# Gated pass of a graph network: the time angle made in turns by TensorE, the features flipped one superblock later

## What is computed

```
# second layer, per edge
ef = jnp.concatenate([h_src, h[col]], axis=1)
edge_weights = jax.nn.sigmoid(jax.nn.relu(ef @ We1 + be1) @ We2 + be2)[:, 0]
aggr = jax.ops.segment_sum(edge_weights[:, None] * h_src, col, num_segments=n)
# fourth layer, per edge
rel_t = last_update[src] - t
rel_t_enc = jnp.cos(rel_t[:, None] * Wt[0][None, :] + bt)
edge_attr = jnp.concatenate([rel_t_enc, msg], axis=-1)
```

## Time and profile before

| what | us |
|---|---|
| median of three runs | 13408.96 |
| lowest and highest run | 13392.93, 13420.43 |
| profiled execution, span | 13400.0 |
| VectorE busy, whole span | 10400.3 (78%) |
| TensorE busy, whole span | 8527.8 (64%) |
| GpSimd busy, whole span | 6926.8 (52%) |
| ScalarE busy, whole span | 3614.6 (27%) |
| gated pass, first to last keeping of the one-hot (L1505) | 6581.2 to 7974.6 |

### The profile page before, as it was taken

How to read it: one execution, slowest core, us unless ns; L and a number is a source line. 1 busy time by engine, 2 the same in 40 slices (tenths; PEclk the granted TensorE clock), 3 DMA queues, 4 the chain that set the end, 5 groups by cost and what they waited for, 6 DMA issues and landing times. The chain is left out here.

```text
span 13400.0 us, 212567 instructions
## 1 busy us (share of the span) xinstructions
PE 8527.8 (64%) x52858; PEld 6962.8 (52%) x52859; DVE 10400.3 (78%) x15015; ACT 3614.6 (27%) x7819; POOL 6926.8 (52%) x7047
## 2 busy tenths in 40 slices
PE   4663477776777677775465652777266666567764
PEld 3553245554455535654455542555266666566664
DVE  8666569974799748996688875888778888688888
ACT  0111133332333233332244431333211111111111
POOL 2775047750477407772277750777145555255553
PEclk8555688877888788887688875666588888788887
DMA  4334754444544474443255550222233334233333
GB/s 182 113 113 119 244 206 106 106 80 193 192 106 106 72 292 123 106 106 53 79 145 145 146 111 19 55 55 54 19 103 106 107 107 105 75 108 105 105 106 72
DMA packets 720185, 1523.62 MB, mean 114 GB/s; under 512 B 364796, under 2 KB 416585, under 8 KB 680627
## 3 DMA queue, kind: packets, MB, share of 16 engines
q0 software_dynamic: 306624, 795.04, 25.0%
q1 hardware_dynamic: 413427, 727.07, 15.9%
HBM read 1050.48 MB, written 471.10 MB: 114 GB/s over the span
## 5 line engine op out<-in xcount | busy, mean ns | idle before, releaser
L970 POOL DMA_INDIRECT h<-table,edges_ring x3984 | 3856.5, 968 | 1889.0 <-issue 1154.3
L1147 PE MATMUL bank<-h,edges_onehot 128*128 128x260 f32 (+1 forms) x7968 | 1986.6, 406 | 652.3 <-issue 469.0
L1147 PEld LDWEIGHTS bank<-h,edges_onehot 128*128 128x128 f32 x7968 | 1570.6, 246 | 978.1 <-issue 717.4
L970 POOL DMA_INDIRECT edges_rows<-table,edges_ring x1512 | 1527.0, 1010 | 716.0 <-issue 431.0
L1122 PE MATMUL bank<-ident,edges_score 128*4 128x128 f32 x5280 | 1027.7, 360 | 1021.5 <-DVE edges_score L1288 737.9
L1258 DVE TENSOR_TENSOR_SCAN bank<-edges_fresh,edges_top,bank 4x1024 f32<-4x1024 bf16 x660 | 1541.5, 2336 | 144.9 <-PE bank L1122 141.2
L1265 DVE TENSOR_TENSOR_SCAN edges_top<-edges_fresh,bank 4x1024 f32<-4x1024 bf16 x660 | 1493.8, 2263 | 0.6 <-issue 0.3
L1122 PEld LDWEIGHTS bank<-ident,edges_score 128*4 128x4 f32 x5280 | 497.6, 104 | 1339.0 <-DVE edges_score L1288 784.9
L1314 DVE TENSOR_TENSOR acc<-acc,bank 128x260 f32 (+1 forms) x2640 | 908.9, 344 | 164.4 <-PE bank L1147 60.4
L2017 POOL DMA_INDIRECT rec<-dst,slots x782 | 797.0, 1019 | 432.7 <-issue 432.4
L1203 ACT ACTIVATE edges_onehotT<-bank 128x1024 bf16<-128x1024 bf16 (+1 forms) x550 | 562.1, 1022 | 1153.3 <-PE bank L1087 715.9
(11 more groups left out here) (346 smaller groups left out, 18152.3 us busy)
## 6 DMA issues: line engine op xcount, KB each, us to landing
table<-x SPq DMA_DIRECT2D x154, 1040.0 KB, 7.9
edge_score<-edge_feat SPq DMA_DIRECT2D x220, 512.0 KB, 3.8
table<-h SPq DMA_DIRECT2D x77, 1040.0 KB, 7.9
table<-source_typed_rows SPq DMA_DIRECT2D x63, 1040.0 KB, 8.1
h<-table,edges_ring POOLq DMA_INDIRECT x3984
edge_feat<-edge_score SPq DMA_DIRECT2D x110, 512.0 KB, 2.9
dst_row<-dst_rows SPq DMA_DIRECT2D x71, 704.0 KB, 4.2
buf<-rec SPq DMA_DIRECT2D x44, 840.0 KB, 5.2
```

The source lines that it names most:

```text
L970: pool.indirect_dma_start(out=rows[s % R][:, j, :], out_offset=None, in_=table, in_offset=bass.IndirectOffsetOnAxis(ap=ring[:, s * ST + j: ...
L1147: ins = pe.matmul(sum_b[k % 3], onehot[s][:, j, :], rows[s][:, j, A0:W], start=j == k * GT, stop=j == (k + 1) * GT - 1)
```

## The change

The turns are now made by TensorE. `rel` gets a ninth column of ones. TensorE flips it (128 x 9 into 9 x 128, L1465), ScalarE keeps it (`relT`, L1534), and one product with nine rows of weights, `angle_w` (9 x 512: Wt/2pi on a block diagonal, and a last row of bt/2pi + 1/4), gives the angle of all eight tiles in turns (L1471). VectorE rounds it (L1609, two additions in one instruction, out of PSUM) and subtracts (L1611, out of PSUM); the fraction goes straight to the sine with a scale just under 2pi (L1545). The angle shares the bank of the one-hot's flip, so the next flip waits for `angle_made` too. The flip of the features and their keeping are moved from step n to step o, one superblock later.

```diff
-        rel, half_pi = p.buffer("rel", (P, ST)), p.buffer("half_pi", (P, 1))
+        rel, relT = p.buffer("rel", (P, ST + 1)), p.buffer("relT", (ST + 1, P))
+        angle_w = p.buffer("angle_w", (ST + 1, ST, 64))
...
+        angle_b, relT_b = flip_b[:, 0:ST * 64], flip_b[0:ST + 1, 512:512 + P]
...
+                def flip_features(o):
+                    u, s = number(o), o[1] % 2
+                    pe.wait_ge(cos_made, u + 1)
+                    pe.wait_ge(message_in[s], 16 * (o[0] * (RING // 2) + o[1] // 2 + 1))
+                    hold(pe, featT_kept, u)
+                    for j in range(ST):
+                        ins = pe.transpose(feat_b[:, j * P:(j + 1) * P], feat[s][:, j, :], g.ident[:, :])
+                    ins.then_inc(feat_flipped, 1)
+                def turn_rel(n):
+                    u = number(n)
+                    pe.wait_ge(flipped_kept, u + 1)
+                    pe.wait_ge(rel_made, u + 1)
+                    park(pe)
+                    pe.transpose(relT_b, rel[:, :], g.ident[:, :]).then_inc(rel_flipped, 1)
+                def make_angle(n):
+                    pe.wait_ge(relT_kept, number(n) + 1)
+                    park(pe)
+                    pe.matmul(angle_b, relT[:, :], angle_w[:, :, :].rearrange("p t k -> p (t k)"), start=True, stop=True
+                              ).then_inc(angle_ready, 1)
...
                         pe.wait_ge(onehot_made, u + 1)
+                        hold(pe, angle_made, u)
                         hold(pe, flipped_kept, u)
...
                     if o:
-                        sum_group(o, 0)
+                        flip_features(o)
                     if n:
                         bins.append(load_bin(pe, g, u, 2))
                     if o:
+                        sum_group(o, 0)
+                    if n:
+                        bins.append(load_bin(pe, g, u, 3))
+                        turn_rel(n)
+                    if o:
                         sum_group(o, 1)
                     if n:
-                        bins.append(load_bin(pe, g, u, 3))
-                    if n:
+                        make_angle(n)
                         pe.wait_ge(flipped_kept, u + 1)
...
+                    if n:
+                        act.wait_ge(rel_flipped, u + 1)
+                        hold(act, angle_ready, u)
+                        act.activation(relT[:, :], relT_b, ACT.Copy).then_inc(relT_kept, 1)
+                    if o:
+                        w, s = number(o), o[1] % 2
+                        act.wait_ge(feat_flipped, w + 1)
+                        hold(act, feat_out[s], 16 * (o[0] * (RING // 2) + o[1] // 2))
+                        act.activation(featT[:, s, :], feat_b[:, :], ACT.Copy).then_inc(featT_kept, 1)
+                    if n:
+                        s = n[1] % 2
+                        act.wait_ge(angle_made, u + 1)
+                        hold(act, feat_flipped, u - 1)
+
+                        act.activation(feat[s][:, :, 0:64], angle[:, :, :], ACT.Sin, scale=UNDER_TWO_PI
+                                       ).then_inc(cos_made, 1)
...
-                        turned = c.mark(v.tensor_tensor(angle[:, :, :], rel[:, :].unsqueeze(2).to_broadcast(wide),
-                                                        wt[:, :].unsqueeze(1).to_broadcast(wide), ALU.mult))
...
+                        v.wait_ge(angle_ready, u + 1)
+                        flat_angle = angle[:, :, :].rearrange("p t k -> p (t k)")
+                        flat_turns = turns[:, :, :].rearrange("p t k -> p (t k)")
+                        c.link(v.tensor_scalar(flat_turns, angle_b, 12582912.0, 12582912.0, ALU.add, ALU.subtract))
+                        hold(v, cos_made, u)
+                        v.tensor_tensor(flat_angle, angle_b, flat_turns, ALU.subtract).then_inc(angle_made, 1)
```

More of the change, by code:

```diff
@@ L54 @@
 TWO_PI = 6.283185307179586
+UNDER_TWO_PI = 6.2831845
 class Chain:
@@ L1472, in step @@
                         sum_group(o, 2)
-                    if n:
-                        pe.wait_ge(cos_made, u + 1)
-                        pe.wait_ge(message_in[s], 16 * (n[0] * (RING // 2) + n[1] // 2 + 1))
-                        hold(pe, featT_kept, u)
-                        for j in range(ST):
-                            ins = pe.transpose(feat_b[:, j * P:(j + 1) * P], feat[s][:, j, :], g.ident[:, :])
-                        ins.then_inc(feat_flipped, 1)
-                    if o:
                         sum_group(o, 3)
@@ L1521, in _ @@
             def _(v):
-                v.memset(half_pi[:, :], TWO_PI / 4).then_inc(chain, 1)
                 v.wait_ge(loaded, 64)
-                C1, C2 = 6.28125, TWO_PI - 6.28125
-                L = 9
-                wide = [P, ST, 64]
+                L = 3
+                wide = [ST + 1, ST, 64]
+                k = Chain(v, chain)
+                v.memset(rel[:, ST:ST + 1], 1.0)
+                v.tensor_scalar(wt[:, :], wt[:, :], 1.0 / TWO_PI, None, ALU.mult)
+                k.link(v.tensor_scalar(bt[:, :], bt[:, :], 1.0 / TWO_PI, 0.25, ALU.mult, ALU.add))
+                k.link(v.tensor_tensor(angle_w[:, :, :], wt[0:ST + 1, :].unsqueeze(1).to_broadcast(wide),
+                                       g.ident[0:ST + 1, 0:ST].unsqueeze(2).to_broadcast(wide), ALU.mult))
+                k.link(v.scalar_tensor_tensor(angle_w[:, :, :], bt[0:ST + 1, :].unsqueeze(1).to_broadcast(wide),
+                                              g.ident[0:ST + 1, ST:ST + 1], angle_w[:, :, :], ALU.mult, ALU.add))
                 def ahead(n):
@@ L1555, in step @@
                         u, s = number(n), n[1]
-                        c = Chain(v, chain, u * L + 1)
+                        c = Chain(v, chain, u * L + 3)
                         v.wait_ge(gathered[s], seen[s] + 16 * ST * (n[0] + 1))
-                        hold(v, cos_made, u)
-                        c.link(v.tensor_tensor(rel[:, :], rows[s][:, :, 2 * D], g.rel_t[:, tiles_of(u)],
-                                               ALU.subtract))
-                        turned = c.mark(v.tensor_tensor(angle[:, :, :], rel[:, :].unsqueeze(2).to_broadcast(wide),
-                                                        wt[:, :].unsqueeze(1).to_broadcast(wide), ALU.mult))
+                        hold(v, rel_flipped, u)
+                        v.tensor_tensor(rel[:, 0:ST], rows[s][:, :, 2 * D], g.rel_t[:, tiles_of(u)], ALU.subtract
+                                        ).then_inc(rel_made, 1)
                     next_bin()
-                    if n:
-                        c.until(turned)
-                        shifted = c.mark(v.tensor_tensor(angle[:, :, :], angle[:, :, :],
-                                                         bt[:, :].unsqueeze(1).to_broadcast(wide), ALU.add))
+                    next_bin()
                     next_bin()
```

49 lines of the change are left out of this document (13 added, 36 removed).

## The result

| | median, us | lowest to highest | ratio, 95% interval |
|---|---|---|---|
| before (4 runs) | 13406.11 | 13392.93 to 13420.43 | |
| changed (4 runs) | 13510.68 | 13504.48 to 13533.81 | 1.0083 (1.0068 to 1.0098) |

A forecast was written before the change was run, and what follows sets the result against it. VectorE bounds the kernel before; the change makes a closed loop: head 6.05 plus tail 5.37 us, plus 2.35 for half clock, rounded to 13.7 against 12.78. Over 109 superblocks +100 us, ends +4: 13513 us, range 13370 to 13640.

The forecast's parts named there:

- VectorE's work: Gated pass: seven VectorE instructions (4.45 us) go, two (1.4 us) come, about 3.1 us less a superblock.
- The tail: VectorE's part of the loop, from addition of the spread to next onehot: 5.37 us, no instruction changed.
- The head at full clock: TensorE's part of the loop, from onehot through flips, sums 0 and 1, angle and spread to VectorE: 6.05 us.
- The half clock: After TensorE's 4.7 us wait, half clock covers 4.7 us of the head and adds 2.35 us a superblock.
- The sum: Gated pass: 109 superblocks at 13.7 instead of 12.78 us, +100 us; with the ends, 13513 us for the kernel.
- The ends: First and last superblock of the pass add 4 us; the one 12.7 us wait for message columns would go.
- Where VectorE waits: In the gated pass, VectorE waits ahead of the rounding (L1609) and of the addition (L1614); busy share about 61%.
- GpSimd: Gathers in the pass: eight take 11.4 us a superblock, no longer than the loop; they get shorter than 1.12 us.
- the prediction's own last sign: Gated pass: the prediction is wrong if VectorE waits for something it has not named.
- Rival 1: TensorE keeps full clock or loses it briefly: loop 11.4 to 11.9 us, kernel 13290 us; chance 0.15.
- Rival 2: Half clock lasts through both flips, both sums and the angle: loop 15.3 us, kernel 13680 us; chance 0.13.
- Rival 4: VectorE stays the bound at 9.7 us a superblock, needing the spread before the angle's product; chance under 0.02.

The follow-up runs named there:

- Experiment 1: Changed kernel with four unread products of 512 columns on TensorE behind sum 3, filling its wait for the one-hot: 13352.21 us, ratio 0.996 to the kernel before.
- experiment 5: Kernel before, angle still on VectorE, with only the flip of the features moved into the head, one superblock later: 13509.92 us, ratio 1.0076.
- Experiment 10: Kernel before with each unused slot's source set to 48 times its partition instead of row 0: 13323.9 us, ratio 0.9939.
- experiment 12: Experiment 7's new order together with Experiment 10's spread sources of unused slots: 13180.17 us, ratio 0.9828 to the kernel before.
- experiment 2: Changed kernel with TensorE's wait behind sum 3 filled by 32 transposes instead of four products: 13339.86 us, ratio 0.995 to the kernel before.
- experiment 6: Changed kernel with the flip of the features moved out of the head, behind sum 3, its keeping behind the sine: 13658.64 us, ratio 1.0182 to the kernel before.
- Experiment 7: Changed kernel reordered: sums 2 and 3, both later-step flips and the angle's product behind the spread: 13273.96 us, ratio 0.9903 to the kernel before.
- experiment 4: Kernel before with two unread products of 512 columns added on TensorE behind sum 3: 13437.51 us, ratio 1.0017.
- experiment 8: Experiment 7 with VectorE's register loads put one each behind long instructions, not three in a row: 13503.3 us, ratio 1.0074 to the kernel before.

## Why the prediction was right

The forecast was 13513 us and slower; measured are 13510.68. The mechanism was in the main the one predicted, and two of its terms were off and cancelled.

- **VectorE's work.** Net 3.1 us less a superblock was right: the two new instructions take 0.69 us each, as taken from L1561, and its share of the pass is 61%, as forecast.
- **The tail** is 5.37 us (7311.39 to the next onehot's end, 7316.76), unchanged.
- **The head at full clock** was forecast as 6.05 us. Experiment 1 has it: from the onehot's end, 7303.49, to the addition, 7310.10, are 6.61 us. The step that failed is the placing of `rel`'s flip. I had counted sum 0 with its 0.47 us; the flip starts 0.86 us behind the start of sum 0 (7306.28 - 7305.42), 0.17 of it a wait "<-issue", which is where TensorE loads a bin number. The order of the instructions ahead of the prediction shows this load, and I gave it no price. The angle's product took 1.03 for 0.93 us. The loop at full clock is 11.95 us and not 11.42.
- **The half clock.** It covers 4.4 us of the head (4.7 forecast), and in the wait it falls 2.2 us in (2.7 forecast): the mean of 0.74 over 4.5 us means that 2.3 of them are at half clock. But it costs 1.7 us and not 2.35. The rule "half the work in that time" failed for sum 0: at half clock it takes from 7306.62 to 7307.48, 0.86 us, about what its four instructions need at the pace of the flips there (0.22 each), and at full clock the same 0.86, for there the load sets it. Only the two flips pay, 0.79 and 0.80 us.
- **The sum.** 13.65 us a superblock against the 13.7 of the forecast. The term head was 0.55 us too small and the term half clock 0.65 too large. That the total fits this closely is luck, the more so as five kernels with other sums settle near 13.65 us (experiment 5); that the loop is a chain of head and tail, with the half clock in the head, is not.
- **The ends.** The wait for the message columns did not go, as I had it: the long step near the end is 6.7 us over the others, 13.0 before. Experiment 10 takes the long step away in the kernel before, and experiment 12 in an order that flips the features one superblock later; neither moves the flip to do so. The columns themselves come late. The first superblock takes 16.82 us, 0.8 more than before.
- **Where VectorE waits.** I named the rounding and the addition, which wait 72.4 us and some 60 in the pass. The most is ahead of the first two takes (397.6 us), since the flip of the features pushes sum 0 back. By the prediction's own last sign, a wait of VectorE that it had not named, this part of the picture was wrong. The wait is in the same chain, ahead of the rounding, and adds nothing to the sum.
- **GpSimd** was no bound. Its gathers fell to 1.08 us from 1.09 and 1.23, as forecast; that it is for the fewer instructions of VectorE beside them isn't shown.

The rivals. Rival 1 (full clock) gives the mechanism its counter-test: experiments 1 and 2 make the full clock by force, and the time is 13352 and 13340 us. The 13290 of the rival lacked the 0.55 us of the head. Rival 2 had the half clock through flips, sums and angle; the changed kernel has it only to the end of sum 0, but experiment 6 shows that a loop of this length exists, at 15.2 us a superblock and 13659 us, against 15.3 and 13680, with the half clock in the sums, the angle and the spread. The rule of the Trainium skill that led there (TensorE: Matmul & The Clock Gate, "Part 4: PE-mode transpose", by which the full clock does not engage for transposes) does not hold for these transposes: in experiment 2 the clock is 1.00 through 3.66 us of nothing else, and with them the loop is as short as with products. Rival 4, VectorE still the bound, wanted the spread ahead of the angle's product. Experiment 7 builds this order and is 237 us faster.

## What to carry to other kernels

When work is taken from the engine that is bound, look first at what chain the new work joins. Here one product that needs 1 us and one flip of 0.9 us were put between the onehot and the spread, on which VectorE's next work waits, and the freed engine only waited longer; with all of it behind the spread the kernel was 1% faster than before. Moving a part alone is no safe step: the flip of the features alone behind the sums made it slower still (experiment 6). A wait that opens on TensorE has a second price, the clock of the work behind it, and it can be read: fill the wait with work that nobody needs, and see what the loop takes. The filling must end before the next needed work, or it measures its own delay (experiment 4).

## What the runs showed of the hardware that I had not expected

- More work on TensorE made a loop faster: four needless products of 512 columns a superblock, 13.65 to 11.95 us, by the granted clock alone (0.75 to 1.00).
- Five kernels, of three orders of the loop, have a median step of 13.64 to 13.66 us, at clocks of 0.75 and 0.76 (experiment 5). Why this length, is open.
- A shorter wait can be worse. With 3.70 us instead of 4.57 the clock fell later, behind the first flip, and 8.5 us of work ran at half clock instead of 4.4.
- A register load takes 0.67 us in a row of three. Behind a long instruction of VectorE it cost next to nothing in the kernel before (0.12 us between L1561 and L1566), and 1.01 and 1.05 us behind the same engine's wait for its own instruction (experiment 8). In the profile it appears only as "<-issue" or as a late releaser.
- Gathers of the stretch where unused slots all read one row took 87.3% of the DMA engines' time for 1.43 MB in 20 us, where the middle of the pass had 27.7% for 1.45 MB, and with spread rows the end had 34.1% for 1.94 MB. Spreading sources that nobody uses was worth 0.6% of the kernel.
